# Heads 4 and 5 of samples 2 to 5 transposed by DMA as well, and four steps around them moved to other places or queues

## The reference, cut to what matters

```python
D, HQ, HK = (128, 32, 8)
PAGES, PSIZE, NPP = (64, 32, 16)
SCALE = 1.0 / float(np.sqrt(D))
# q, k = rope(rmsnorm(x @ Wq.T)), rope(rmsnorm(x @ Wk.T)); v = x @ Wv.T
# per head: probs = softmax(q @ k.T * SCALE + mask); out = (probs @ v) @ Wo.T, summed over heads
```

## Time and profile before

| | us |
|---|---|
| three runs, median (lowest to highest) | 1299.64 (1299.5 to 1300.43) |
| the profiled execution | 1296.74 |
| its span | 1295.1 |
| PE busy in the span | 1277.9 (99%) |
| DVE, ACT, POOL busy | 935.0, 784.7, 768.0 |

### The profile page before, as it was taken

One profiled execution on the slowest core, in us unless ns is written; L12 is line 12 of the kernel. 1 busy time (PEld: TensorE's weight loads), 2 busy tenths in 40 slices (PEclk: granted clock), 3 DMA queues, 4 the chain that ended last, 5 costly groups with the idle time before them and its releaser, 6 DMA issues.

```text
span 1295.1 us, 26067 instructions
## 1 busy us (share of the span) xinstructions
PE 1277.9 (99%) x6698; PEld 1092.6 (84%) x6698; DVE 935.0 (72%) x2658; ACT 784.7 (61%) x1834; POOL 768.0 (59%) x792
## 2 busy tenths in 40 slices
PE   9999999999999999999999999999999999999998
PEld 8888877887888888888888888888888888888886
DVE  6532457778777777877777788777777977777774
ACT  6731334556666668676666676766656767656664
POOL 2110011348766668787666697866667869666663
PEclk9999999999999999999999999999999999999999
DMA  8321224176655558756555677655556775555543
GB/s 295 103 82 49 73 71 142 55 268 193 130 126 131 129 124 214 185 125 142 129 130 126 133 205 190 126 131 135 132 132 160 185 186 132 125 124 124 124 96 82
DMA packets 314896, 179.57 MB, mean 139 GB/s; under 512 B 260418, under 2 KB 279234, under 8 KB 314562
## 3 DMA queue, kind: packets, MB, share of 16 engines
q1 hardware_dynamic: 295840, 125.83, 40.8%
q0 software_dynamic: 12032, 35.40, 10.4%
q10 hardware_dynamic: 6946, 17.44, 4.4%
HBM read 119.71 MB, written 16.91 MB: 105 GB/s over the span
## 4 chain that ended last, share of the span: by engine, by line
PE 78%; SPq 7%; issue 5%; DVE 4%; POOL 2%; DMA 2%; ACT 1%; POOLq 0%; DVEq 0%; ACTq 0%
PE bank L1624 15%; PE tail L1662 13%; PE wide L1692 12%; PE tail L1729 10%; PE wide L464 4%; PE wide L1656 4%; PE wide L544 3%; PE bank L1645 3%; PE bank L464 3%; PE tail L464 3%; SPq L1513 2%; SPq L1527 2%; PE wide L599 2%; SPq L1552 2%; DMA turned<-parts 1%
## 5 line engine op out<-in xcount | busy, mean ns | idle before, releaser
L1662 PE MATMUL tail<-prT,vt 128*128 128x512 f32 x960 | 258.5, 409 | 0.7 <-POOL prT L1410 0.5
L1662 PEld LDWEIGHTS tail<-prT,vt 128*128 128x128 f32 x960 | 172.0, 190 | 40.4 <-DVE prT L2077 10.0
L1343 POOL TENSOR_TENSOR tick<-tick 128x1 f32<-128x1 f32 x254 | 57.9, 228 | 220.7 <-PE tail L1662 77.0
L1729 PE MATMUL tail<-woT,oT 128*128 128x512 f32 x768 | 179.5, 389 | 0.9 <-DVE oT L2129 0.9
L1729 PEld LDWEIGHTS tail<-woT,oT 128*128 128x128 f32 x768 | 144.0, 188 | 31.2 <-DVE oT L2129 1.3
L1692 PE MATMUL wide<-kT,qT 128*128 128x320 f32 x512 | 158.7, 310 | 1.8 <-DVE mx L2105 1.5
L1692 PE MATMUL wide<-kT_low,qT 128*128 128x320 f32 x512 | 158.2, 309 | 0.0
L1692 PE MATMUL wide<-kT,qT_low 128*128 128x320 f32 x512 | 157.9, 308 | 0.0
L1401 POOL TENSOR_TENSOR parts<-raw,parts 128x1280 f16<-128x1280 f32 x55 | 145.7, 2648 | 8.0
L1874 ACT ACTIVATE raw<-raw,nm,q_scale 128x640 f32<-128x640 f32 x124 | 114.6, 924 | 46.6 <-DVE nm L2108 45.0
L1874 ACT ACTIVATE pr<-pr,nm,q_scale 128x640 f32<-128x640 f32 x128 | 117.9, 921 | 35.7 <-DVE nm L2108 34.9
(11 more groups left out here) (289 smaller groups left out, 2852.4 us busy)
## 6 DMA issues: line engine op xcount, KB each, us to landing
w_ring<-pair_weights SPq DMA_DIRECT2D x80, 256.0 KB, 3.9
k_raw<-k_pages SPq DMA_DIRECT2D x512, 32.0 KB, 1.7
v_raw<-v_pages SPq DMA_DIRECT2D x512, 32.0 KB, 2.8
spread<-one_over_denominators ACTq DMA_DIRECT2D x32, 512.0 KB, 4.8
xTb<-x_transposed POOLq DMA_DIRECT2D x31, 512.0 KB, 4.1
rope<-rope_tables SPq DMA_DIRECT2D x31, 256.0 KB, 2.7
out<-y POOLq DMA_DIRECT2D x31, 256.0 KB, 5.4
w_raw<-w_gate_up SPq DMA_DIRECT2D x10, 512.0 KB
```

The source lines that it names most:

```text
L1343: nc.gpsimd.tensor_tensor(tick[:, 2:3], tick[:, 1:2], tick[:, 1:2], ALU.add).then_inc(s_carry, 1)
L1662: last = nc.tensor.matmul(tail[g][:, :], vt[v_part][:, j, g * D:(g + 1) * D], prT[p_part][:, :, j, :], start=(j == v_part == p_part == 0), ...
L1729: last = nc.tensor.matmul(place[:, :], oT[:, g, o_part, (h % REP) * S:(h % REP + 1) * S], woT[w_part][:, h, :], start=(h == o_part == w_pa ...
```

## The change

- In turns whose back unit is of samples 2 to 5 (`has_third`, 16 of 32 units), heads 4 and 5 go by DMA as well: POOL splits them (`halve_third`), SP issues two more transposes (`turn_third`), ACT copies the high part (`high_turned_third`) and POOL the low part (`low_turned_third`). PE, ACT and DVE handle only heads 6 and 7 of the probabilities there.
- The next x is loaded by a DMA of ACT instead of POOL, ahead of `store_shares`.
- In the 16 turns, `spread_shares` comes after the high part of the keys, `add_share` after `split_keys`, `share_room` between the two `halve`s, and 14 of the 16 value pages after the new transposes; two key pages go behind the first transpose.
- PE's wait for the low parts (`s_tl`) moves behind the high sums of group 0; ACT takes a wait for them ahead of the high part of the first queries. In the one turn without an output share (unit 1), group 0 is summed by pairs of heads (`by_pairs`).
- In the 16 turns, PE's sums of group 1 come as all ten with high parts, then the five with low parts.

```diff
-    pr = [place(135168 + h * 2560 if h < 6 else 163840 + (h - 6) * 2560, f"pr{h}", [P, NK]) for h in range(REP, HP)]
+    pr_third = place(145408, "pr_third", [P, HALF, NK])
+    pr = [pr_third[:, h, :] for h in range(HALF)] + [place(163840 + h * 2560, f"pr{REP + HALF + h}", [P, NK]) for h in range(HALF)]
-    spread = place(135168, "spread", [P, G, REP * S])
+    turned_third = [place(145408 + i * 2560, f"turned_third{i}", [P, HALF * JT, S], F16)[:, :, :] for i in range(2)]
+    spread = place(140288, "spread", [P, G, REP * S])
...
+    THIRDS = range(2, 6)
+
+    def has_third(b):
+
+        return b in THIRDS if isinstance(b, int) else True
+
+    def thirds(pair, b):
+
+        done = min(max(b - THIRDS[0], 0), len(THIRDS)) if isinstance(b, int) else b - THIRDS[0]
+        return done + pair * len(THIRDS)
...
-            with eng.Fori(0, B - 3) as last:
-                turn(pair, last + 2, before(last + (pair * B + 2)), True, True, True, None, True, True)
+            turn(pair, 2, before(pair * B + 2), True, True, True, None, True, True)
+            with eng.Fori(0, len(THIRDS) - 1) as last:
+                turn(pair, last + 3, before(last + (pair * B + 3)), True, True, True, None, True, True)
+            turn(pair, 6, before(pair * B + 6), True, True, True, None, True, True)
...
+        def halve_third(u, before, n):
+
+            pool.wait_ge(s_exp, u * HP + 3 * HALF)
+            for i in range(2):
+                pool.wait_ge(s_turned[0][i], (u + before) * 16 + 16)
+            carry(n)
+            nc.gpsimd.tensor_copy(parts[0][:, 0], pr_third[:, :, :]).then_inc(s_half, 1)
+            pool.wait_ge(s_half, u * 2 + before + 3)
+            nc.gpsimd.tensor_tensor(parts[0][:, 1], pr_third[:, :, :], parts[0][:, 0], ALU.subtract).then_inc(s_rest[0], HALF)
+
+        def low_turned_third(u, before, n):
+
+            pool.wait_ge(s_turned[0][1], (u + before) * 16 + 32)
+            pool.wait_ge(s_pv, u * G + 1 + FIRST)
+            carry(n)
+            nc.gpsimd.tensor_copy(prT[1][:, 0:HALF].rearrange("p h j q -> p (h j) q"), turned_third[1]).then_inc(s_tl, 1)
...
-            if then_x is not None:
-                pool.wait_ge(s_q1, u + 1)
-                carry(n)
-                if first_turn:
-                    pool.wait_ge(s_xs[0], 16 * BLK)
-                load_x(then_x)
-                n = n + 1
-            if share is not None:
+            if share is not None and not has_third(b - 1):
                 add_share(u - 2, share, n)
                 n = n + 1
             if not first_turn:
                 pool.wait_ge(s_rope, u * G + G + FIRST)
                 split_keys(u, n)
                 n = n + 1
+            if has_third(b - 1):
+                low_turned_third(u - 1, thirds(pair, b - 1), n)
+                add_share(u - 2, share, n + 1)
+                n = n + 2
...
-            share_room(u, share is not None)
+            if not has_third(b - 1):
+                share_room(u, share is not None)
...
-                halve(u, n + 1, 0, False, extra != "next")
-                halve(u, n + 2, 1, False, then_x is not None and extra != "next")
+                halve(u, before, n + 1, 0, False, extra != "next")
+                if has_third(b - 1):
+                    share_room(u, True)
+                halve(u, before, n + 2, 1, False, then_x is not None and extra != "next")
+                if has_third(b):
+                    halve_third(u, before, n + 3)
+                    n = n + 1
...
+        def turn_third(pair, b):
+
+            u, before = unit(pair, b), thirds(pair, b)
+            sp.wait_ge(s_rest[0], (u + before) * HALF + 2 * HALF)
+            for i in range(2):
+                sp.sem_inc(s_seen, 1)
+                sp.dma_start_transpose(turned_third[i], parts[0][:, i].rearrange("p h n -> p (h n)")).then_inc(s_turned[0][i], 16)
+
...
+            if has_third(b - 1):
+                load_rope(pair, b)
+                load_keys(pair, b, pages, 0, NPP - 2)
+                turn_part(pair, b - 1, 0, 0)
+                load_keys(pair, b, pages, NPP - 2)
+                turn_part(pair, b - 1, 0, 1)
+                turn_part(pair, b - 1, 1, 0)
+                turn_part(pair, b - 1, 1, 1)
+                load_values(pair, b, pages, 0, VALUES_FIRST)
+                turn_third(pair, b - 1)
+                load_values(pair, b, pages, VALUES_FIRST)
+            else:
...
-                return [pr[i][:, j * P:(j + 1) * P] for i in range(REP)]
+                return [pr[i][:, j * P:(j + 1) * P] for i in range(HALF if third else 0, REP)]
...
-            if back:
-                pe.wait_ge(s_tl, u * 2 + 2)
+            by_pairs = front and back and not share
             if front:
 
                 pe.wait_ge(s_step, n * NSTEP + TURNED)
                 transposes(1, [ra[:, i, :] for i in range(REP)])
             if back:
-                for k in range(2):
-                    pe.wait_ge(s_th[k], u + 1)
+                pe.wait_ge(s_th[0], u + before_back + 1)
+                if not by_pairs:
+                    pe.wait_ge(s_th[1], u + 1)
                 pe.wait_ge(s_vs, u + 1 + FIRST)
                 pe.wait_ge(s_o, u * G + FIRST)
-                highs = sums(0, range(JT), (0, 1), 0)
-                if front:
-                    sums(0, (0, 1), (0,), 1)
+                if by_pairs:
+                    sums(0, range(JT), (0, 1), 0, 0, HALF)
+                    pe.wait_ge(s_tl, u * 2 + before_back + 1)
+                    sums(0, range(JT), (0,), 1, 0, HALF)
+                    pe.wait_ge(s_th[1], u + 1)
+                    sums(0, range(JT), (0, 1), 0, HALF)
+                else:
+                    highs = sums(0, range(JT), (0, 1), 0)
+                low_heads = HALF if by_pairs else 0
+                if third:
+                    pe.wait_ge(s_rope, n * G + 2 + FIRST)
+                    transposes(0, [ra[:, REP + i, :] for i in range(G)])
+                    probs_wide(1, 0)
+                    pe.wait_ge(s_tl, u * 2 + before_back + 2)
+                    sums(0, range(JT), (0,), 1).then_inc(s_pv, 1)
+                    probs_wide(1, 1)
+                elif front:
+                    pe.wait_ge(s_tl, u * 2 + before_back + 2)
+                    sums(0, (0, 1), (0,), 1, low_heads)
                     if not share or shares_first:
                         begin(0)
                     probs_wide(1, 0)
                 else:
                     highs.then_inc(s_ph, 1)
+                    pe.wait_ge(s_tl, u * 2 + before_back + 2)
                     sums(0, range(JT), (0,), 1).then_inc(s_pv, 1)
             if front:
                 if not back:
                     rest.fourth_quarter()
-                pe.wait_ge(s_rope, n * G + 2 + FIRST)
-                transposes(0, [ra[:, REP + i, :] for i in range(G)])
-            if back and front:
-                sums(0, (2, 3), (0,), 1)
+                if not third:
+                    pe.wait_ge(s_rope, n * G + 2 + FIRST)
+                    transposes(0, [ra[:, REP + i, :] for i in range(G)])
+            if back and front and not third:
+                sums(0, (2, 3), (0,), 1, low_heads)
                 if second_queries_late(pair, b, front, back):
                     pe.wait_ge(s_second_root, second_queries_late(pair, b, front, back) * ROOT_STEPS)
                 probs_wide(1, 1)
...
-                sums(0, (JT - 1,), (0,), 1).then_inc(s_pv, 1)
+                if not third:
+                    sums(0, (JT - 1,), (0,), 1, low_heads).then_inc(s_pv, 1)
                 transposes(0, probs_of(1, JT - 1))
-            if back:
+            if third:
+                pe.wait_ge(s_yadd, u + FIRST)
+                pe.wait_ge(s_th[0], u + before_back + 2)
+                for w in range(2):
+                    pe.wait_ge(s_phi, u * 3 + w + 1)
+                    sums(1, (2 * w, 2 * w + 1), (0, 1), 0)
+                pe.wait_ge(s_phi, u * 3 + 3)
+                sums(1, (JT - 1,), (0, 1), 0)
+                for w in range(2):
+                    pe.wait_ge(t_free[w], u + 1 + FIRST)
+                pe.wait_ge(s_tl, u * 2 + before_back + 3)
+                sums(1, range(JT - 1), (0,), 1)
+                begin(0)
+                sums(1, (JT - 1,), (0,), 1).then_inc(s_pv, 1)
...
+            def load_x(b):
+
+                act.dma_start(xTb[:, :, :, :].rearrange("p i k c -> p (i k c)").bitcast(F32),
+                              x_scratch[bass.ds(b, 1)].rearrange("o p n -> (o p) n")).then_inc(s_xt, 16)
...
+            def high_turned_third():
+
+                act.wait_ge(s_turned[0][0], (u + before_back) * 16 + 32)
+                ac.copy(prT[0][:, 0:HALF].rearrange("p h j q -> p (h j) q"), turned_third[0]).then_inc(s_th[0], 1)
...
-                act.wait_ge(s_turned[0][1], u * 16 + 16)
+                act.wait_ge(s_turned[1][1], u * 16 + 16)
...
+                if ahead:
+                    load_x((b + 1) % B if isinstance(b, int) else b + 1)
...
```

(43 more changed lines are left out.)

158 lines of the change are left out of this document (87 added, 71 removed).

## The result

The changed kernel takes 1323.41 us (median of 4, 1321.68 to 1327.26), the kernel before, run beside it, 1299.57: ratio 1.0188, 95% interval 1.0166 to 1.021. It is slower by 24 us where 18 less was forecast, and lies outside the range of 1276 to 1290. The profiled execution took 1323.87 us.

The account below looks back on a forecast made before the run. PE was taken to bound the kernel, busy 1277.9 of 1295.1 us. Savings of 17.4 (transposes) and 2.0 (moved wait) less 1.6 (ACT) make 17.8, so 1299.64 becomes 1281.8, rounded to 1281.5; range 1276 to 1290.

Parts of the forecast that it names:

- SP and its DMAs: SP's queue in turns with thirds: two more transposes, later value and key pages all arrive in time; nothing charged.
- My POOL sum: POOL's steps from `split_values`: third split at t 4.9 of the next turn, low copies in time; nothing charged.
- The rival of the loop: POOL, transposes and value pages close too slowly, 31.3 against 30.0 at a landing of 5.0: 1291 us; chance 0.14.
- The x load on ACT: One more issue of 0.39 on ACT moves `high_turned` to t 6.1, done at 7.4 against 8.6: hidden, 1.2 to spare.
- PE's own work: Turns with thirds lose 10 of 20 probability transposes at 0.109 each: 1.09 per turn, 17.4 us over 16 turns.
- The moved wait: PE's wait for POOL's low copies, now behind ten high sums: 2.0 us come back at units 10 and 18.
- The wait of 1.2 for `q_scale` at unit 8: PE arrives 1.00 earlier and stands 1.20 for `q_scale`; no gain there or at units 16, 24 and 1.
- ACT's chain: ACT's five steps from keys' high copy to first high part: 0.2 room, 0.1 per turn charged (1.6 us), bound 0.5.
- The spread: Spread DMA issued at 11.3 instead of 8.4, landing after 4.6 where 6.3 is allowed before the mask; nothing charged.
- The sum: Whole-kernel gain 17.4 + 2.0 - 1.6 = 17.8 us, taking the median from 1299.64 to 1281.8, rounded to 1281.5.
- the spread's sum: In that step, the first mask's time: scores at 17.4 plus 0.88 was given as 18.4.

Follow-up runs that it names:

- e8: Changed kernel with only the load of x issued later, behind the cast of the second queries: 1310.0 us, ratio 1.0075.
- e1: Changed kernel with eight value pages instead of two issued by SP before it waits for the third: 1296.0 us, ratio 0.9971.
- e3: Kernel before with only x's load moved from POOL's queue to ACT's, right behind the second squares: 1307.0 us, ratio 1.0063.
- e4: Changed kernel with SP loading key pages two at a time, same bytes, half the issues, wrong output: 1284.8 us, ratio 0.9878.
- e11: As e10, but ScalarE copies the output's share behind the second squares instead of ahead of them: 1280.2 us, ratio 0.9848.
- e12: As e11, but x issued some 2 us later, behind the cast of the new keys: 1286.1 us, ratio 0.9883.
- e10: Changed kernel with eight value pages first and x issued ahead of the cast of the second queries' first half: 1286.1 us, ratio 0.9905.

## Why the prediction was wrong

**The step that failed** is "SP and its DMAs ... Nothing charged". Three things were wrong in it and in the rival beside it.
- I walked SP once, from the third transposes to the first transpose of the next turn, and stopped at "ends at about 24", because the data were ready at 23.7. I never went on through the transpose (0, 1) and its landing to the split of the third. The third shares `parts[0]`, which is free only when (0, 1) has landed. My POOL sum put that split straight behind the other two (34.9, t 4.9). The profile has POOL idle there, 1.70 at 952.12. The rival of the loop went through POOL and the value pages, was priced at a landing of 5.0, and got 0.14; the loop that closed needs only the 3.5 of the earlier trace rows.
- The round by my own rows is 2.7 + 6.7 + 8.6 to the first transpose (fourteen key pages), 1.4 for it, 1.1 for two pages, 3.5, 0.3 and 4.1: 28.4 of 30.0. So even the whole walk would have left 1.6 us of room, and the charge of nothing rested on issue costs that I had too low. Measured the round is 31.5. Of the 3.1 between, the page numbers' register load, which I had left out, is 1.0. The rest is spread: key pages 8.33/14 = 0.59 instead of 0.57, value pages 6.88/14 = 0.49 instead of 0.48, and some 0.2 at each change of kind.
- The lateness adds up over a sample's turns, as that rival said, and surfaces as PE waits of up to 3.5 us. The longest in the list, 4.2 at unit 18, is x's (e8).

By e1 this step is worth 28 us of the 42 between forecast and result. What a wait costs is more than its length where PE's clock falls after it, as the last section shows; the sum had no term for that.

**"The x load on ACT ... hidden, with 1.2 to spare"** counted the 0.39 of issue and not the 512 KB. It is 8 us on the kernel before (e3) and 24.4 - 9.8 = 14.6 on the changed one (e8), half of it in unit 18's turn of the profiled execution. In e4, with room on SP's queue, it cost PE next to nothing. My rule for a moved step, that its DMA counts too, I applied to SP's queue alone.

**PE's own work** was right: 384 matmuls at the probability transposes, and turns of 29.9 where nothing holds PE up (e4), 1.21 less than 31.08 where I said 1.09 less 0.1. The Trainium skill's 275 ns for a transpose (TensorE: Matmul & The Clock Gate, Part 4: PE-mode transpose) would have made it an estimated 2.75 less; the measured turn decides against it as a price in a stream.

**The moved wait**: 2.0 forecast, 4.2 [1.6, 6.6] measured; right within what can be told. The wait of 1.2 for `q_scale` at unit 8 came out at 1.21 with that edit alone. In the whole change it is 1.62, with 0.34 for `ra` ahead of it; the four such units lose some 3 us more than the forecast had. e11 takes a part of it back by an edit of ACT's order.

**ACT's chain**: the 0.1 per turn does not show (29.87 to 29.91 in e4, without a wait of PE for ACT's high copies); e12 shows that one issue of 0.4 in it costs the 0.5 that I gave as its bound.

**The spread** held nothing up. No run sets its landing alone, so the rule cited from the Trainium skill on completion counts (DMA: Bandwidth & Descriptors, Queues, rings and completion order) is neither shown nor refuted. The landings that grew (a transpose beside x, e3 and e10) would fit it and would also fit plain sharing of the DMA engines.

**The sum** (1281.8 before it was rounded to 1281.5; in the spread's sum 18.4 should read 18.3) is not confirmed to the microsecond. With the two failed steps repaired, e10 is at 1286.1, 12.3 below the kernel before where 17.8 were forecast, and e4, with one of them repaired, at 15.9 below. e11's 1280.2 is near the 1281.5 partly by luck: it has an edit that the forecast did not have.

## What to carry to other kernels

Where a queue issues work that waits for an engine that waits for that queue's own earlier work, write the round out as a closed loop and divide it by the period: every issue, every register load, every landing, and the buffer that the next round reuses. If it comes close to the period (here 28.4 of 30.0 by the rows, and 31.5 when run), put independent issues in front of the blocking one, as many as fill the pause. Moving a large DMA moves its bytes: look at which small, awaited transfers are under way at the new moment, and at its consumer, before calling it hidden.

## What the chip showed besides

PE's clock fell after some stalls. At unit 8 PE waits for `q_scale` in e4 and in e10, nearly as long. In e4's timeline a first stall stands ahead of it; under it is the window view from 531 to 534 (last columns: granted clock, DMA share, GB/s):

```profile
528.73 0.44 PE L1717 MATMUL bank<-ident,ra 128*128 128x128 f32 x2 [0.34 <-DVE ra L2197]
...
531.25 0.69 PE L1728 MATMUL wide<-ident,pr_third 128*128 128x128 f32 x2 [1.63 <-DVE q_scale L2185]
531.73 0.63 PE L1728 MATMUL wide<-ident,pr 128*128 128x128 f32 x2
532.16 0.64 PE L1728 MATMUL wide<-ident,pr_third 128*128 128x128 f32 x2
```

```profile
531.00:534.00 3.00, 2.75 (x13) 2.75 (x14) 2.35 (x5) 0.19 (x1) 1.77 (x2) 0.51 0.89 289
```

And in e10, where only the one stall stands:

```profile
531.63 0.44 PE L1728 MATMUL wide<-ident,pr_third 128*128 128x128 f32 x2 [1.57 <-DVE q_scale L2185]
531.91 0.38 PE L1728 MATMUL wide<-ident,pr 128*128 128x128 f32 x2
532.13 0.38 PE L1728 MATMUL wide<-ident,pr_third 128*128 128x128 f32 x2
```

```profile
531.00:534.00 3.00, 2.37 (x19) 2.25 (x20) 2.84 (x8) 0.80 (x2) 2.15 (x2) 1.00 0.90 312
```

With a granted clock of 0.51, the 1.2 GHz level, two transposes take 0.43 us, at 1.00 they take 0.22, and the turn is 35.04 us in e4 and 32.87 in e10. Against the 31.08 of a plain turn, e4's is 3.96 longer with stalls of 1.97, e10's 1.79 longer with one of 1.57. So where the clock falls, such a stall can cost some 2 us more than itself.

The first stall is not what decides it. The changed kernel has the same two at unit 8, 0.34 and 1.62, and its clock held:

```profile
538.51 0.44 PE L1728 MATMUL wide<-ident,pr_third 128*128 128x128 f32 x2 [1.62 <-DVE q_scale L2185]
```

```profile
538.00:541.00 3.00, 2.48 (x19) 2.35 (x20) 2.85 (x7) 0.92 (x2) 1.89 (x1) 1.00 1.08 314
```

At unit 24 of the same execution it fell, to 0.57 over 3 us, after a stall of again 1.62. What decides was not found.

In the changed kernel the mean granted clock is 0.992 over the span and PE is busy for 1273.8 us; in e10, with the same instructions on PE, it is 0.999 and 1260.2. These 13.6 us are where the part of the 17.4 went which its busy time did not show. For example, the ten sums behind the stall of 3.50 in unit 14's turn took 3.93 us with a granted clock of 0.52, where ten take 2.56 at 1.00.
